# Attention of a graph layer: a group's tile of node rows is copied to a fixed place by ScalarE instead of being addressed through a register by TensorE

## The reference, cut to what matters

```
h = (x @ W.T).reshape(n, H, D)                      # H = 8 heads of D = 32
alpha = sum(h[src] * a_src) + sum(h[dst] * a_dst)   # per edge and head
enc = relu(edge_attr @ edge_W.T + edge_b)
alpha = alpha + sum(enc * h[dst], axis=-1)
alpha = where(alpha >= 0, alpha, 0.2 * alpha)
ex = exp(alpha - segment_max(alpha, dst)[dst])
attn = ex / segment_sum(ex, dst)[dst]
out = segment_sum(h[src] * attn, dst) + bias
```

## Time and profile before

| what | value |
|---|---|
| median of three timed runs | 2692.37 us (2689.56 to 2695.32) |
| profiled execution, span from first to last instruction | 3020.7 us |
| PE busy | 2056.3 us, 68% |
| DVE busy | 1662.5 us, 55% |
| POOL busy | 1243.1 us, 41% |
| ACT busy | 817.2 us, 27% |
| attention in the profile | about 1676 to 2556 us |

### The profile page before, as it was taken

The page is one execution under the profiler, slowest core; times in us unless marked ns, Lnnn a source line. Parts: engine busy times, 40 slices in busy tenths (PEclk is TensorE's granted clock), DMA queues, the critical chain, the costliest instruction groups (busy, mean ns, idle before and its releaser), DMA issues. The chain is left out here.

```text
span 3020.7 us, 41561 instructions
## 1 busy us (share of the span) xinstructions
PE 2056.3 (68%) x12513; PEld 1558.0 (52%) x12602; DVE 1662.5 (55%) x3351; ACT 817.2 (27%) x2162; POOL 1243.1 (41%) x1222
## 2 busy tenths in 40 slices
PE   3364555555559996699713477777777776996995
PEld 1243444443437775599702255555555554335995
DVE  7444444443438768655478377677767677403222
ACT  7222222222210002133313223232233232432331
POOL 0466656666640000255402565566666661001221
PEclk9667777777779998799956688888888897997998
DMA  2344443333358861422231344444444443300113
GB/s 74 106 157 143 153 141 137 137 138 136 135 201 293 292 236 54 162 72 71 75 101 53 120 129 120 123 127 126 124 124 127 122 129 96 110 9 23 36 38 104
DMA packets 192122, 366.15 MB, mean 121 GB/s; under 512 B 47573, under 2 KB 102632, under 8 KB 191525
## 3 DMA queue, kind: packets, MB, share of 16 engines
q1 hardware_dynamic: 135472, 207.05, 21.2%
q0 software_dynamic: 56160, 156.43, 16.6%
q10 hardware_dynamic: 274, 0.00, 0.0%
HBM read 232.23 MB, written 131.07 MB: 120 GB/s over the span
## 5 line engine op out<-in xcount | busy, mean ns | idle before, releaser
L1929 POOL DMA_INDIRECT att_rows<-hdram,top_ix x488 | 513.9, 1053 | 322.7 <-issue 308.8
L839 POOL DMA_INDIRECT mtab<-first_w,msgs_ix x308 | 306.9, 996 | 186.6 <-issue 92.0
L708 PE MATMUL msgs_p_m<-nodes_n,msgs_hott 128*128 x976 | 351.5, 522 | 46.4 <-issue 33.3
L2001 PE MATMUL att_p_acc<-att_msg,att_hot 128*128 128x264 f32 x976 | 304.5, 466 | 71.5 <-ACT att_msg L2039 31.0
L708 PEld LDWEIGHTS msgs_p_m<-nodes_n,msgs_hott 128*128 128x128 f32 x976 | 244.7, 263 | 108.1 <-issue 64.2
L2001 PEld LDWEIGHTS att_p_acc<-att_msg,att_hot 128*128 128x128 f32 x976 | 210.6, 227 | 127.6 <-issue 61.3
L2031 ACT ACTIVATE att_enc<-att_p_z 128x1024 f32<-128x1024 f32 x122 | 124.8, 1023 | 538.8 <-DMA exp_rows<-ntab,ffn0x_gat 263.5
L2108 DVE TENSOR_TENSOR att_enc<-att_enc,att_p_h 128x1024 f32<-128x1024 f32 x122 | 148.8, 1220 | 216.8 <-DMA exp_rows<-ntab,ffn0x_gat 132.2
L1341 PE MATMUL exp_y<-exp_own,exp_ht 128*128 128x256 f32 x1032 | 239.0, 379 | 2.4 <-issue 2.4
L1953 PE MATMUL att_p_h<-heads_parts,att_hz 128*128 x1464 | 203.9, 293 | 43.5 <-DVE att_enc L2108 30.1
L607 DVE TENSOR_TENSOR first_w<-msgs_p_m,msgs_sorted 128x1024 f32<-128x1024 f32 x77 | 94.2, 1224 | 243.3 <-remote 112.6
(11 more groups left out here) (383 smaller groups left out, 3866.4 us busy)
## 6 DMA issues: line engine op xcount, KB each, us to landing
first_w<-mtab SPq DMA_DIRECT2D x77, 520.0 KB
etab<-msgs_et SPq DMA_DIRECT2D x122, 288.0 KB
att_hz<-etab SPq DMA_DIRECT2D x122, 288.0 KB
msgs_rw<-mtab SPq DMA_DIRECT2D x45, 520.0 KB, 4.6
first_w<-in_L_ffn_w SPq DMA_DIRECT2D x16, 512.0 KB
ffn0x_w<-in_L_ffn_w SPq DMA_DIRECT2D x16, 512.0 KB
ffn_w<-in_L_ffn_Wd SPq DMA_DIRECT2D x8, 1024.0 KB
att_rows<-hdram,top_ix POOLq DMA_INDIRECT x488
```

The lines of the kernel that those rows point to most:

```text
L708: last = T.matmul(p_m[g % 2][:, q, :], hott[g % 2][:, q, :], node, start=True, stop=True)
L839: nc.gpsimd.indirect_dma_start(mtab, bass.IndirectOffsetOnAxis(ap=ix[:, g, q:q + 1], axis=0), rw[g % RS][:, q, :], None).then_inc(s_free[g ...
L1929: nc.gpsimd.indirect_dma_start(rows[:, g % RS, q, :], None, hdram, bass.IndirectOffsetOnAxis(ap=ix1[:, g, q:q + 1], axis=0)).then_inc(s_ro ...
L2001: last = T.matmul(p_acc[g % 2][:, 0:HW], hot[g % 2][:, q, :], msg[g % 2][:, q, :], start=(q == 0), stop=(q == G - 1))
```

## The change

Before it handles group g, ScalarE reads the tile number into a register of its own and copies the 792 bf16 numbers per partition of that tile from `hparts` to one of two fixed places, `node[g % 2]`. The matmuls of L1953 and L1963 read that place. The two places are memory that two earlier tiles no longer need (a weight and the logits), so nothing new is allocated. A new semaphore `s_node` tells TensorE that the copy is there; ScalarE waits for `s_adst` before it writes over a place. The copies of groups 0 and 1 come before the first relu; the copy of group s + 2 comes in step s behind `encodings(s + 1)`, ahead of `copy_back`, `falls`, `exponents` and `weights`.

```diff
+    node = [lent.bitcast(BF16)[:, 0:3 * HN].rearrange("p (k c) -> p k c", k=3) for lent in spare]
@@ TensorE
             def destinations(g):
-                b = pe.value_load(gb[0:1, g:g + 1], min_val=0, max_val=NT - 1)
-                node = hparts[:, bass.ds(b, 1), :, :].rearrange("p a k c -> p (a k) c")
+                pe.wait_ge(s_node, g + 1)
                 if g:
                     pe.wait_ge(s_prod, g)
                 for q in range(G):
                     for k in range(3):
-                        last = T.matmul(p_h[:, q, :], hott_of(g, q), node[:, k, H:HN], start=(k == 0), stop=(k == 2))
+                        last = T.matmul(p_h[:, q, :], hott_of(g, q), node[g % 2][:, k, H:HN], start=(k == 0), stop=(k == 2))
@@
-                        last = T.matmul(p_adst[:, c * H:(c + 1) * H], hott_of(g, q), node[:, k, 0:H],
+                        last = T.matmul(p_adst[:, c * H:(c + 1) * H], hott_of(g, q), node[g % 2][:, k, 0:H],
@@ ScalarE
+            def own_tile(g):
+                b = act.value_load(gb[0:1, g:g + 1], min_val=0, max_val=NT - 1)
+                if g >= 2:
+                    act.wait_ge(s_adst, g - 1)
+                S.copy(node[g % 2][:].rearrange("p k c -> p (k c)"),
+                       hparts[:, bass.ds(b, 1), :, :].rearrange("p a k c -> p (a k c)")).then_inc(s_node, 1)
@@
+            own_tile(0)
+            own_tile(1)
             encodings(0)
             widen(0)
             for s in range(NG + LAG + 3):
                 t, j = s // BG, s % BG
                 if s + 1 < NG:
                     encodings(s + 1)
+                if s + 2 < NG:
+                    own_tile(s + 2)
                 if j == 0 and 0 < t <= NB:
                     copy_back(t - 1)
@@ build
-                    attention(nc, ..., hparts, hdram, acc)
+                    attention(nc, ..., hparts, hdram, acc,
+                              [wts["wn"][:].rearrange("p k c -> p (k c)"), logits[:].rearrange("p t e -> p (t e)")])
```

More of the change, by code:

```diff
@@ L1855, in split, with attention @@
     link(V.tensor_copy(parts[2], rest))
-def attention(nc, a, cst, etab, segtab, ewz, ix1, penn, gb, keep, hparts, hdram, acc):
+def attention(nc, a, cst, etab, segtab, ewz, ix1, penn, gb, keep, hparts, hdram, acc, spare):
     RS, SE = 12, 10
@@ L1889, in attention @@
     (s_z, s_enc, s_h, s_prod, s_red, s_adst, s_al, s_line, s_chain, s_rb, s_back, s_backc, s_top, s_new, s_fall, s_edge,
-     s_dif, s_ex, s_msg, s_wide, s_acc, s_add, s_go, s_weight, s_kept) = (a.sem(m) for m in (
+     s_dif, s_ex, s_msg, s_wide, s_acc, s_add, s_go, s_weight, s_kept, s_node) = (a.sem(m) for m in (
          "z", "enc", "h", "prod", "red", "adst", "al", "line", "chain", "rb", "back", "backc", "top", "new", "fall", "edge",
-         "dif", "ex", "msg", "wide", "acc", "add", "go", "weight", "kept"))
+         "dif", "ex", "msg", "wide", "acc", "add", "go", "weight", "kept", "node"))
     s_rows, s_hz, s_seg = ([a.sem(f"{m}{s}") for s in range(k)] for m, k in (("rows", RS), ("hz", SE), ("seg", 2)))
@@ L1952, in destinations, with offsets @@
                     for k in range(3):
-                        last = T.matmul(p_h[:, q, :], hott_of(g, q), node[:, k, H:HN], start=(k == 0), stop=(k == 2))
+                        last = T.matmul(p_h[:, q, :], hott_of(g, q), node[g % 2][:, k, H:HN], start=(k == 0), stop=(k == 2))
                 last.then_inc(s_h, 1)
-                return node
-            def offsets(g, node):
+            def offsets(g):
                 if g >= BG:
@@ L2005, in _ @@
             encoders(0)
-            node = destinations(0)
+            destinations(0)
             for s in range(NG + LAG + 3):
@@ L2011, in _ @@
                 if s < NG:
-                    offsets(s, node)
+                    offsets(s)
                 if s + 1 < NG:
                     encoders(s + 1)
-                    node = destinations(s + 1)
+                    destinations(s + 1)
                 if j == 0 and 0 < t <= NB:
@@ L2261, in build @@
                 with ExitStack() as c1:
-                    attention(nc, Pool_(nc, c1, "att"), cst, etab, segtab, ewz, ix1, penn, gb[1], buckets[1], hparts, hdram, acc)
+                    attention(nc, Pool_(nc, c1, "att"), cst, etab, segtab, ewz, ix1, penn, gb[1], buckets[1], hparts, hdram, acc,
+                              [wts["wn"][:].rearrange("p k c -> p (k c)"), logits[:].rearrange("p t e -> p (t e)")])
             reuse_semaphores(nc)
```

## The result

The changed kernel takes 2687.2 us (median of 20 runs, 2682.7 to 2692.8), the kernel before beside it 2693.9 us (20 runs, 2689.6 to 2697.8). The ratio is 0.9976 [0.9970, 0.9983]: 6.6 us faster. Two later measurements of the changed kernel gave 0.9969 [0.9958, 0.9981] and 0.9977 [0.9962, 0.9992]. Forecast was 2704 us, slower; the time lies in the range, the direction is wrong.

What follows compares the result with a forecast made beforehand. In attention, DVE's turn (20.3 us with gaps) was taken as the bound, ScalarE's loop becoming longer by 0.3. Registers -2.4, copy +9 and disturbances +5 gave about +12 on 2692.4: 2704 us, range 2676 to 2748.

Steps and rivals of the forecast that it cites:

- What bounds the kernel: Attention stage: 880 us profiled, 663 to 880 timed, without stalls before DVE's product; nearer DVE's floor than the profile shows.
- DVE floor: Attention: DVE's own work, 612.4 us busy, 20.1 us per turn of four groups, some 20.3 with gaps.
- Part 1, registers: TensorE loses its register load and instructions before L1953 and L1963: 2.4 us gain, bounds 0 and 29.6.
- C: Rival: TensorE's register work is on the path more than seen; faster, mid value -15, 2677 us; chance 0.23.
- Part 2, the copy: ScalarE gains a 0.84 us copy per group, pushing what follows back by 0.74 us; price 9 us.
- the loop: Relu, weights, sums and next step's encoders, closed through ScalarE and PE: 17.6 us a turn before, 20.6 after.
- A: The forecast case: the loop on ScalarE is just the longer one, +12 us (+6 to +30); chance 0.35.
- The 9 us: Price of the copy in attention: loop of 20.6 us against DVE's 20.3, times 30.5 turns; bounds nothing and 18.
- B: Rival: the copy lies in ScalarE's idle time, nothing to be measured; 2692 us, within 5; chance 0.28.
- The disturbances: Attention: lost slack to take up disturbances at a granted clock of 0.85; 5 us, could be 90.
- D: Rival: late semaphores or lower clock in timed runs too, most copies exposed; +45, 2737 us; chance 0.14.

Runs made afterwards that it cites:

- the second profile: The kernel before, with no edit, timed and profiled again: 2696.0 us, ratio 0.9998 [0.9985, 1.0011]; profiled span 2694.6 us.
- The fixed tile: The kernel before with TensorE reading tile 0 for every group, without load, register instructions or copy: 2695.9 us, ratio 1.0003 against the kernel before.
- the hold out of the way: Message's second operand read from PSUM instead of SBUF: 2676.1 us in the changed kernel, 2668.0 us in the kernel before.
- the memset's kernel: The kernel before with an unread 96-column memset on DVE ahead of the message in each turn's first step: 2694.8 us, ratio 1.0001.

## Why the prediction was wrong

**What bounds the kernel: here it failed.** "The timed attention ... stands nearer to its DVE floor" took DVE's turn, 20.1 us busy and 20.3 with its gaps, for the bound. The earlier trace rows have POOL at 513.9 us, and its row in that profile is

```profile
L1929 POOL DMA_INDIRECT att_rows<-hdram,top_ix x488 | 513.9, 1053 | 322.7 <-issue 308.8 <-DVE att_enc L2108 12.6 <-POOLq L1408 1.2
```

405 of the 487 gaps between gathers are 0.30 us there too. 513.9 us and 488 gaps of 0.30 us are 660 us, against 612 on DVE and about 675 for the whole stage in the second profile. The gaps were not added, because a stage of 880 us left room for both. The inference that timed runs lack the stalls was right (216.8 us then, 15.6 now), and so was 663 us as its lower end; but with the room gone another engine was the last.

**Part 1, registers: size right.** Taken 2.4 us, bounds 0 and 29.6. The fixed tile gives 1.0003 [0.9994, 1.0012], so C, the case that had the faster side, is false, although the direction that it gave is the one that came. No row of the changed kernel shows the wait for `s_node` releasing anything, as predicted. The rule of the Trainium skill on the queue of 64 (TensorE: Matmul & The Clock Gate, "Architectural detail: the array is 16× 32×32, not 1× 128×128") gave 0, and the run agrees with it, though none shows a queue's depth.

**Part 2, the copy.** Its duration, 0.84 us, is 0.843 measured, 122 times; it starts 0.92 us behind the relu (1734.41 to 1735.33, changed kernel):

```profile
1734.41 1.02 ACT L2030 ACTIVATE att_enc<-att_p_z 128x1024 f32<-128x1024 f32 x1 [2.24 <-PE att_p_z L1943]
...
1735.33 0.84 ACT L2036 COPY wts_logits<-heads_parts 128x792 bf16 x1
...
1736.07 0.25 ACT L2045 COPY att_msg<-att_ex 128x32 f32<-128x32 f32 x1
...
1736.58 2.02 PE L2000 MATMUL att_p_acc<-att_msg,att_hot 128*128 128x264 f32 x8 [0.89 <-ACT att_msg L2045]
...
1738.43 0.27 PE L1969 MATMUL att_p_top<-top_ident,att_al 128*128 128x128 f32 x1
...
1738.81 0.42 DVE L2139 TENSOR_TENSOR_SCAN att_run<-att_seg,att_p_top 128x128 f32<-128x128 bf16 x1 [0.61 <-PE att_p_top L1969]
...
1739.48 1.22 DVE L2167 TENSOR_TENSOR att_msg<-att_rows,att_ex 128x1024 f32<-128x1024 f32 x1
```

The weights start 0.74 us behind the copy, the sums 0.51 us behind those: the loop is as predicted. Forecast for the wait for the weights was 60 us or more; 56.2 were measured, against 1.0. Its price was put at 9 us against a DVE floor. With the hold out of the way that is what it costs: 8.2 us (7.0 by the two ratios), and nothing when the copy stands behind the cast. There the gathers' turn is 615.1/30.5 = 20.2 us, shorter than the loop of 20.6. So A's mechanism and size are right for a kernel without the hold. In this kernel GpSimd binds: DVE waits 35 us for rows anyway, and a loop of 20.6 us fits in a turn of 650.4/30.5 = 21.3 us. The 9 us are the term that failed: nothing of them is to be seen, and the kernel is 6.6 us faster. B had the price right (nothing), but for ScalarE's idle time and without the gain.

**What none of the cases had: the sign.** The same rows show the path. With the loop late, the transpose of L1969 comes late at the first step of a turn, DVE stands 0.61 us before the scan, and the message behind it starts later. Over the stage this wait is 6.0 us in 11 turns, against 1.7 us in the unchanged kernel. It moves the first message of those turns against the train of gathers, one each 1.25 us. Yet those turns aren't the ones that save: in the changed kernel's profile the ten first messages behind such a wait (and with gathers still running) are held 0.58 us in the mean, the other 19 are at 0.46. The other four kernels with the delay have the same order (0.67, 0.54, 0.73 and 0.57 against 0.41, 0.34, 0.30 and 0.26). If the delay shortens the hold, then in other turns than those it strikes.

Shown: the gain is the delay that the copy puts on ScalarE's work (alone 0.9979, moved behind the cast 1.0006), copies in steps 1 to 3 are enough for it (0.9981), and with messages that don't hold gathers the same delay is a loss. Seen together with it in ten profiles: gathers that are 4.7 us shorter, all of it at the first step. Not shown: that these shorter gathers are the gain (the memset's kernel has them without it), and why the first message meets fewer gathers. The cause of the faster side stays open. No case of the prediction had a way to it, and that the time fell into the range is luck. The few tenths by which messages move against gathers look like chance of this schedule, not like a rule.

The prediction's own sign for C was also misleading: "faster by over 5 us" was to mean that the register work was on the path. The kernel is 6.6 us faster, the idle time before L1953 went from 4.8 to 3.2 us only, and the fixed tile gains nothing.

**The disturbances** (5 us, and D). D's condition, stalls as in the earlier trace rows in timed runs, is real on one chip, and there the copy in three of four steps costs 0.6%; where the forecast was timed it isn't there. The 5 us leaned on a clock of 0.85; it was 0.97 in the second profile of the kernel before and 0.96 in the changed one, with 43 us more idle ahead of the sums, 0.35 us per group. So neither the 5 us nor D's fall of the clock appears. The rule of the Trainium skill on pauses (TensorE: Matmul & The Clock Gate, "Why this matters for your kernels") is about longer ones than these and isn't tested by them.

## What to carry to other kernels

For every engine add up busy time and the fixed gaps between its instructions before naming a bound: a row with idle time equal to its count times one constant is an engine that never waits. Where GpSimd issues gathers without a pause, look at what DVE's instructions with both operands in SBUF do to their durations; an operand moved to PSUM was worth 27 us, four times the change under study. A gain of 0.2% from added work can be a matter of phase, that is, of which instructions happen to meet, and it should be tried with the work somewhere else in the order before it is believed.

## What the runs showed of the hardware

In the unchanged kernel's second profile a gather issued by GpSimd took 0.946 us, with 0.30 us to the next. When it started 0.033 to 1.07 us into a DVE multiply of 1024 elements with both operands in SBUF, it ended 0.81 to 0.82 us after that multiply, up to 1.06 us late (99 gathers). Started within 0.031 us of the multiply's start, it wasn't held (9 gathers). A short multiply does the same, by less: in the kernel with the exponents in PSUM the 23 gathers that start during the one of 264 elements (0.43 us, both operands in SBUF) end 0.82 us behind it and last 0.97 to 1.17 us. The 0.43 us spread of bf16 numbers says nothing on this: its 7 gathers started within 0.01 us of its start.

The Trainium skill offers a cause (SBUF — State Buffer, "🔬 SBUF: two separate sides"): DVE and GpSimd share a port pair under an exclusive lock. A DVE instruction with two SBUF inputs contends for it with a GpSimd instruction that reads SBUF; the one that starts first has it for its whole length and the other is blocked. The 2.00 us against 0.95 us above agree with it, and so do the nine gathers that weren't held. The other half doesn't show: 98 of the 122 messages started while a gather was running, and no message lasted more than 1.286 us, against 1.218 in the median. No run shows the lock itself.

The stalls in front of the product (3.03 us in the earlier trace rows) came back on one chip: 232.0 us before the product, and 3026.7 us for the kernel before. On another chip the idle time before the product is 15.6 us, and the kernel before takes 2694 us there. The cause of the stalls wasn't tried.
